# Masks of the first scores as two constant operand rows and triangles of 64; first loads dealt anew; new orders

## The chip, the cores and the metric

The kernel runs on one core of a Trainium2 chip. The metric is the device time of one execution in microseconds (us), the median of three runs. The engines are TensorE (PE, matrix products), VectorE (DVE), ScalarE (ACT), GpSimd (POOL) and SyncE (SP), which here only issues transfers.

## The reference

Four residual steps on x of 4 batches x 256 tokens x 128 features:

```python
x = x + tanh(g_xattn[0]) * xattn0(layernorm(x), ctx, ctx, ...)   # 16 heads of 8, masked
x = x + tanh(g_ffn[0])   * ffn0(layernorm(x), ...)               # top-1 of 6 low-rank token factors
x = x + tanh(g_xattn[1]) * xattn1(layernorm(x), ctx, ...)        # 8 heads of 64
x = x + tanh(g_ffn[1])   * ffn1(layernorm(x), ...)               # top-2 of 8 experts, then a layer norm
```

The change touches the mask of the first attention. A token sees only tokens before it, and token 0 sees itself:

```python
scores = jnp.einsum('bihd,bjhd->bhij', qh, kh) * scale
keep = (j < i) | (i == 0) & (j == 0)
scores = jnp.where(keep, scores, jnp.float32(-jnp.inf))
probs = jax.nn.softmax(scores, axis=-1)
```

## The kernel before

Each engine runs a list written out by hand: `PE_ORDER`, `ACT_ORDER`, `DVE_ORDER`, `POOL_ORDER` and `SP_ORDER`. An entry such as `S:6` names a function and its arguments. An engine takes its list strictly in order and waits on semaphores where data or a buffer is missing.

PSUM has three pairs of banks that are used in turn by the entries in `PAIRED` (projections `pk`, keys and values `kv`, scores `S`, transposed scores `T` and others), so an entry waits until the entry three places before it in that ring has been read. One bank (`misc`) serves transposes and small products, one the attention outputs.

The first attention works like this. `xT:0:b` transposes the normalised x of batch b, `pk:b` projects the context to keys and values, `pq:b` the queries. Queries and keys are split in three bf16 parts each (`hi`, `sres`, `mid`, `lo`), so that a float32 product becomes one bf16 product over six planes of 8 features, 48 rows (`KR`). The parts go through a scratch tensor in memory: `so:b:part` on SP writes them (two transfers for each part), `si:b` waits for all of them and reads them back as one head per block of columns, eight heads on rows 0 to 47 and eight on rows 64 to 111.

Scores are computed twice. First `S:n`, 24 groups, six for each batch (`UNITS`): rows are queries, and VectorE (`mx:n`) takes the negated row maxima out of them. For this pass TensorE first writes the mask into the diagonal block of each bank, as an identity times a mask tile (line 1092), and adds the score products on top (line 1097). Groups with it=1 hold the queries 128 to 255 (two heads of 256 columns in a bank, two masks of 256 columns), groups with it=0 the queries 0 to 127 (four heads of 128 columns, two masks of 512 columns). `mparts:b` splits the maxima in two bf16 parts, `mT:b` transposes them, `MTc:b` copies them, and two transfers (`shift:b` on SP, one on ACT) put them in as two more operand rows, 48 and 49; the keys have rows of ones there. Then `T:n:i` (lines 1112 and 1116) computes the transposed scores with the maxima subtracted, ScalarE exponentiates (`e0`), GpSimd zeroes the masked triangle (`mask:n`), and `AV:n` multiplies with the values.

`hT`, `oT` and `wo0` carry the heads to the output projection, `awo0` adds to x. The first feed-forward runs over `gate`, `yk`, `ym` (mask times factors), `lg` (logits), `pte`, `U` and `val`; the second attention over `q`, `sc`, `tp` and `av1`, with keys and values from the context by `kv:b:0` and `kv:b:1`; the experts are `hid` and `eo`.

SP loads x, the context and weights at the start, ACT the constants and the small tables of the first feed-forward (`COL`, `BTG`, `WTD`, `AA`, `BW`).

Of the kernel before, what the change touches and what calls it, by code (L numbers as in the profile page):

```python
# [34 lines left out]
KS = KR + 2  # L35
# [9 lines left out]
C_ID, C_MASK, C_W6 = 0, 128, 384  # L45
NCONST = 390
# [10 lines left out]
xT:0:0 pk:0 pq:0 xT:0:1 pk:1 pq:1 tok:0 kv:0:0 xT:0:2 kv:0:1 pk:2 pq:2 xT:0:3 pk:3 pq:3 kv:1:0 kv:1:1 S:0 S:1  # L57
S:2 S:3 S:4 S:5 kv:2:0 S:6 S:7 mT:0 S:8 S:9 kv:2:1 S:10 T:0:0 S:11 T:0:1 T:1:0 T:1:1 S:12 mT:1 AV:0 T:2:0 T:2:1
S:13 AV:1 S:14 T:3:0 T:3:1 hT:0 AV:2 S:15 T:4:0 S:16 AV:3 T:4:1 S:17 T:5:0 hT:1 T:5:1 T:6:0 S:18 S:19 mT:2 AV:4
T:6:1 S:20 oT:0 T:7:0 S:21 wo0:0 T:7:1 AV:5 T:8:0 S:22 T:8:1 AV:6 T:9:0 hT:2 T:9:1 S:23 xT:1:0 AV:7 gate:0  # L60
T:10:0 T:10:1 AV:8 T:11:0 hT:3 yk:0 mT:3 AV:9 tok:1 oT:1 lg:0 T:11:1 wo0:1 kv:3:0 hT:4 pte:0 T:12:0 AV:10 xT:1:1
# [62 lines left out]
def build_program(nc, x, ctxT, w0, wo0, btg, aa, wtd, vecs, cols, w1, wo1, wr, bias, w12, consts,  # L124
# [6 lines left out]
    with ctx:  # L131
# [20 lines left out]
        MSKB = sb("MSKB", [P, 2, P], bf16)  # L152
# [21 lines left out]
        ONE = sb("ONE", [2, S], bf16)  # L174
# [100 lines left out]
        d_one, s_one = map(sem, ("d_one", "s_one"))  # L275
# [48 lines left out]
        def _(sp):  # L324
# [80 lines left out]
        def _(pool):  # L405
# [4 lines left out]
            g_.memset(ONE[:, :], 1.0).then_inc(s_one, 1)  # L410
# [82 lines left out]
        def _(act):  # L493
# [86 lines left out]
            def maxima_rows(b):  # L580
# [385 lines left out]
        def _(pe):  # L966
# [113 lines left out]
            def scores0(n):  # L1080
# [20 lines left out]
            def scores0T(n, i):  # L1101
# [299 lines left out]
```

## Time and profile before

| | |
|---|---|
| median of the runs | 204.18 us (203.66 to 204.18) |
| the profiled execution, its own time | 204.24 us |
| its span, first to last instruction | 202.2 us |
| busy: PE, DVE, ACT, POOL | 181.8, 142.5, 122.7, 105.4 us |
| chain that ended last, by engine | PE 60%, DVE 19%, DMA 5%, ACT 4% |

The profile is one execution. Busy is the time in which an engine had an instruction running; matmuls are pipelined, so a busy TensorE is not one at its peak. In the views a row gives the start in us from the span's beginning, the busy time, engine, line of the kernel, operation, the tile written and read with shapes, the number of instructions, and in brackets how long the engine had been idle before, and what released it.

### The profile page before, as it was taken

The page shows a single profiled execution, that of the slowest core. Times are in us where ns is not written, and L with a number is a line of the kernel's source. Part 1 is how long each engine was busy: PE and PEld are TensorE (multiplying, and loading weights), DVE is VectorE, ACT ScalarE, POOL GpSimd, SP SyncE. Part 2 cuts the span into 40 slices and gives each one's busy share as a digit, 9 for nine tenths or more (in the row PEclk, how much of TensorE's full clock was granted, in tenths as well). Part 3 has the DMA queues.
Part 4 walks back from the last instruction along what each step waited for, and adds up shares of the span by engine and source line. Part 5 has one row for each costly group of instructions (what it writes and reads, how often), then busy time and mean ns, then how long its engine had stood idle before and what let it go on. Part 6 is the DMA issues. An engine that isn't in the chain of part 4 may idle for free.

```text
span 202.2 us, 4352 instructions
## 1 busy us (share of the span) xinstructions
PE 181.8 (90%) x1516; PEld 128.4 (64%) x1516; DVE 142.5 (70%) x361; ACT 122.7 (61%) x313; POOL 105.4 (52%) x153
## 2 busy tenths in 40 slices
PE   0799789799999999999898999999999899999990
PEld 0588244254456857465675877667867679998980
DVE  1684499877996465678878585795798755857744
ACT  0665402777687795676795568788776737255250
POOL 7420000275457446594555938896695955095302
PEclk9999999999999999999999999999999999999999
DMA  5968994854000000000000000000006107347101
GB/s 97 342 188 228 284 206 104 243 132 63 8 5 0 3 3 0 0 3 0 3 0 3 0 3 0 0 3 0 0 2 181 58 3 233 110 130 200 60 26 52
DMA packets 14744, 15.04 MB, mean 74 GB/s; under 512 B 1695, under 2 KB 12164, under 8 KB 14724
## 3 DMA queue, kind: packets, MB, share of 16 engines
q1 hardware_dynamic: 13676, 14.28, 26.4%
q10 hardware_dynamic: 1048, 0.50, 1.1%
q8 instruction: 12, 0.20, 0.4%
q14 instruction: 8, 0.07, 0.1%
HBM read 10.98 MB, written 3.67 MB: 72 GB/s over the span
## 4 chain that ended last, share of the span: by engine, by line
PE 60%; DVE 19%; DMA 5%; ACT 4%; SPq 3%; POOL 3%; issue 3%; POOLq 0%; DVEq 0%; ACTq 0%
PE PS L1319 7%; PE PS L1329 7%; DVE MX L754 6%; PE PS L1135 6%; PE PS L1258 6%; PE PS L1287 5%; PE PS L1271 4%; DMA POOLED<-qk_scr 3%; ACT POOLED L650 3%; PE PS L1092 3%; PE PS L1299 3%; DVE XH L722 3%; DVE NM L857 2%; SPq L352 2%; DMA W<-in_w 2%
## 5 line engine op out<-in xcount | busy, mean ns | idle before, releaser
L458 POOL TENSOR_TENSOR POOLED<-POOLED,RC 128x512 f32<-128x512 f32 x32 | 32.8, 1047 | 13.9 <-DVE RC L866 13.9
L650 ACT ACTIVATE POOLED<-PS,NM 128x256 f32<-128x256 f32 x64 | 29.4, 480 | 7.0 <-DVE NM L857 5.1
L754 DVE TENSOR_REDUCE MX<-PS 128x4 f32<-128x1024 f32 (+1 forms) x24 | 28.5, 1221 | 6.8 <-PE PS L1097 6.6
L447 POOL TENSOR_SCALAR_AFFINE_SELECT PT<-PT 128x512 f32<-128x512 f32 x16 | 10.2, 638 | 41.0 <-ACT PT L570 41.0
L570 ACT ACTIVATE PT<-PS 128x768 f32<-128x768 f32 x32 | 24.8, 809 | 4.8 <-PE PS L1116 4.7
L857 DVE TENSOR_REDUCE NM<-PS 128x4 f32<-128x1024 f32 x16 | 19.4, 1218 | 3.5 <-PE PS L1258 3.2
L722 DVE TENSOR_SCALAR XH<-X,MV,RS 128x128 f32<-128x128 f32 x32 | 15.8, 536 | 4.8 <-POOL RS L416 4.8
L681 ACT ACTIVATE POOLED<-PS,BI 128x256 f32<-128x256 f32 x32 | 12.6, 475 | 10.7 <-PE PS L1319 8.7
L1258 PE MATMUL PS<-KT,VA 64*128 64x256 f32 x128 | 17.9, 400 | 0.1
L415 POOL TENSOR_SCALAR VE<-MV 128x2 f32<-128x2 f32 x20 | 5.3, 267 | 24.2 <-DVE MV L707 12.9
L1271 PE MATMUL PS<-CST,POOLED 128*128 128x128 f32 x128 | 17.1, 276 | 0.1
L1287 PE MATMUL PS<-POOLED,V 128*64 128x256 f32 x128 | 16.6, 389 | 0.0
L1271 PEld LDWEIGHTS PS<-CST,POOLED 128*128 128x128 f32 x128 | 14.1, 141 | 3.2 <-issue 2.3
L1329 PEld LDWEIGHTS PS<-POOLED 128*128 128x128 f32 x128 | 14.8, 192 | 1.4 <-issue 1.1
L1329 PE MATMUL PS<-POOLED 128*128 128x128 f32 x128 | 15.6, 278 | 0.2
L416 POOL TENSOR_TENSOR RS<-VE,HALF 128x2 f32<-128x2 f32 x20 | 14.6, 731 | 1.7
L1319 PE MATMUL PS<-XT,POOLED 128*128 128x256 f32 x64 | 14.9, 382 | 0.0
L1135 PE MATMUL PS<-PT,VA 128*32 128x256 f32 (+1 forms) x256 | 13.8, 331 | 0.0
L1033 PE MATMUL PS<-CST,XH 128*128 128x128 f32 x32 | 7.0, 303 | 7.6 <-DVE XH L722 6.7
L650 ACT ACTIVATION_READ_ACCUMULATOR POOLED<-PS,NM 128x1 f32 x64 | 13.6, 212 | 0.0
L1258 PEld LDWEIGHTS PS<-KT,VA 64*128 64x128 f32 x128 | 11.2, 186 | 3.5 <-issue 1.9
L1092 PE MATMUL PS<-MSKB,IDB 128*128 128x256 bf16 (+1 forms) x48 | 11.1, 312 | 2.3 <-DMA POOLED<-qk_scr 1.2
(146 smaller groups left out, 383.1 us busy)
## 6 DMA issues: line engine op xcount, KB each, us to landing
POOLED<-in_w SPq DMA_DIRECT2D x8, 512.0 KB, 4.0
POOLED<-qk_scr SPq DMA_DIRECT2D x8, 384.0 KB, 6.0
qk_scr<-POOLED SPq DMA_DIRECT2D x8, 192.0 KB, 2.4
qk_scr<-POOLED SPq DMA_DIRECT2D x8, 128.0 KB, 2.2
W<-in_w SPq DMA_DIRECT2D x3, 256.0 KB, 5.8
BI<-in_bias SPq DMA_DIRECT2D x8, 66.0 KB, 3.7
qk_scr<-POOLED SPq DMA_DIRECT2D x8, 64.0 KB, 2.6
out_x<-X SPq DMA_DIRECT2D x4, 128.0 KB, 1.8
```

Of the source, the lines that this page charges most:

```text
L458: g_.tensor_tensor(pr, pr, RC1[:, n % 2, 2 * h:2 * h + 2].unsqueeze(2).to_broadcast([P, 2, S]), ALU.mult).then_inc(s_p1p, 1)
L570: a.activation(PT0[:, n % 3, i:4:2, :], pair("T", n, i).rearrange("p (r n) -> p r n", r=2)[:, :, 0:384], ACT.Exp, scale=D0 ** -0.5).then_i ...
L650: last = a.activation(PR[n % 3][:, h, it, :], pair("sc", n)[:, h * 512 + it * S:h * 512 + (it + 1) * S], ACT.Exp, bias=NM1[:, n % 2, 2 * h ...
L722: last = v.tensor_scalar(XH[:, t, :], X[:, t, :], MV[:, t, 0:1], RS[:, t:t + 1], ALU.subtract, ALU.mult)
L754: v.tensor_reduce(MX0[:, b, it, :, hw * k:hw * (k + 1)], pair("S", n).rearrange("p (r h j) -> p r h j", r=2, h=hw), AXX, ALU.max, negate=T ...
L857: v.tensor_reduce(NM1[:, k, :], pair("sc", n).rearrange("p (c j) -> p c j", j=S), AXX, ALU.max, negate=True).then_inc(s_nm1, 1)
L1135: last = mm(banks(6)[rows, half + jt * P:half + S], VA[:, 2 * b + jt, 4 * hg + g, :], src, start=(jt == 0), stop=(jt == 1), skip_group_che ...
L1258: last = mm(bank[:, h * 512 + it * S:h * 512 + (it + 1) * S], QT1[rows, b % 2, c, it * P:(it + 1) * P], KT1[rows, c, b * S:(b + 1) * S], s ...
L1271: last = nc.tensor.transpose(bank[:, at:at + P], PR[n % 3][:, h, it, jt * P:(jt + 1) * P], ident)
L1287: last = mm(banks(6)[rows, (n % 2) * S:(n % 2 + 1) * S], V1[:, 2 * b + jt, (2 * c + h) * D1:(2 * c + h + 1) * D1], PT1[n % 3][:, h, jt, :] ...
L1319: last = mm(bank[:, f * S:(f + 1) * S], W12[m][:, f * P:(f + 1) * P], XT[:, b * S:(b + 1) * S], start=True, stop=True)
L1329: last = mm(bank[:, 512 * t:512 * t + P], HT[:, m % 2, f, t * P:(t + 1) * P], W12[m][:, F + f * P:F + (f + 1) * P], start=(f == 0), stop=( ...
```

## The change

Five things are done.

1. The mask of the first scores is no longer a full 128 x 128 block on the diagonal. Only the two triangles of 64 on the diagonal are added by products with an identity (64 rows each, the two banks of a pair taking rows 0 to 63 and 64 to 127; `SHIFTED` is the identity with its halves swapped). The 64 x 64 square above the diagonal between them is masked by two further operand rows of the scores: on the query side ones in a quarter of the tokens, on the key side -1e30 in the next quarter. The score products so have 50 rows (`KM`) in place of 48, the transposed ones 52 (`KS`) in place of 50. The maxima move to rows 50 and 51.
2. These rows and the rows of ones come from a new tensor in memory, `rows`, by four transfers (`constant_rows`); before, two transfers took the ones from a tile that GpSimd had set.
3. ACT starts with two loads in place of eight. The mask constants go to SP (`cm`), the tables of the first feed-forward to SP after the output weights (`te`). W0 goes ahead of the context, x:1 behind the first of the key and value weights, W1:0 and the last context ahead of the first scratch read.
4. The orders of all five engines are new.
5. The ODT copy of batch 0 waits for `COL` itself, since `COL` is now loaded late.

```diff
+KM = KR + 2
+KS = KM + 2
+HP = P // 2
...
+            def constant_rows():
+                for side, n in ((1, 4), (0, 2)):
+                    for r in range(2):
+                        sp.dma_start(BIGF[64 * r + KR:64 * r + KR + n, 4096 * side:4096 * (side + 1)].rearrange(
+                            "p (b n) -> p b n", b=B),
+                            rows[side, 0:n].unsqueeze(1).to_broadcast([n, B, H0 * S // 4])).then_inc(d_one, 16)
...
+                a.activation(SHIFTED[:, 0:HP], ident[:, HP:P], ACT.Copy)
+                a.activation(SHIFTED[:, HP:P], ident[:, 0:HP], ACT.Copy)
...
-                for r in range(2):
-                    diag = bank[:, r, :].rearrange("p (h j) -> p h j", h=hw)[:, :, w - P:w]
-                    mm(diag, IDB[:, :], MSKB[:, it:it + 1, :].to_broadcast([P, hw, P]),
-                       start=True, stop=False, skip_group_check=True)
+                for half in range(2):
+                    for r in range(2):
+                        rows = slice(HP * r, HP * (r + 1))
+                        part = bank[:, r, :].rearrange("p (h j) -> p h j", h=hw)[:, :, w - P + HP * half:w - HP + HP * half]
+                        which = MSKB[rows, max(it, half):max(it, half) + 1, :].to_broadcast([HP, hw, HP])
+                        mm(part, (IDB, SHIFTED)[(half + r) % 2][rows, :], which, start=(half == 0), stop=False,
+                           skip_group_check=True)
                 for g in range(hw):
                     for r in range(2):
-                        rows = slice(64 * r, 64 * r + KR)
+                        rows = slice(64 * r, 64 * r + KM)
...
+    for k in range(2):
+        half[0, k] = np.where(quarter == 2 * k, one, 0)
+        half[1, k] = np.where(quarter == 2 * k + 1, low, 0)
...
-x:0 x:1 c:0 w0 x:2 c:1 w1:1 w1:2 c:2 so:0:0 so:0:1 so:0:2 so:1:0 so:1:1 so:1:2 si:0 so:2:0 so:2:1 so:2:2 si:1
+x:0 w0 c:0 cm w1:1 x:1 w1:2 x:2 one c:1 so:0:0 so:0:1 so:0:2 w1:0 c:2 si:0 so:1:0 so:1:1 so:1:2 so:2:0 so:2:1
```

Three places of the lists, as the built programs have them. First SP from its start to the first scratch read, before and then after. `qk_scr` is the scratch tensor, `CT` the context, a `W` of 384 columns W0 and one of 512 a part of W1.

```order
L330 DMA X<-in_x 128x2x128 x2
L333 DMA CT<-in_ctxT 128x256
L336 DMA W<-in_w 128x384
L330 DMA X<-in_x 128x4x128
L333 DMA CT<-in_ctxT 128x256
L339 DMA W<-in_w 128x512 x2
L333 DMA CT<-in_ctxT 128x512
L352 DMA qk_scr<-POOLED 128x3x256 x2
L352 DMA qk_scr<-POOLED 128x2x256 x2
L352 DMA qk_scr<-POOLED 128x256 x2
...
L361 DMA POOLED<-qk_scr 48x2x2048 x2
```

```order
L347 DMA POOLED<-in_rows 4x4x1024 x2
L347 DMA POOLED<-in_rows 2x4x1024 x2
L335 DMA CT<-in_ctxT 128x256
L366 DMA qk_scr<-POOLED 128x3x256 x2
L366 DMA qk_scr<-POOLED 128x2x256 x2
L366 DMA qk_scr<-POOLED 128x256 x2
L341 DMA W<-in_w 128x512
L335 DMA CT<-in_ctxT 128x512
L375 DMA POOLED<-qk_scr 48x2x2048 x2
```

Before, the writes of batches 0 and 1, twelve transfers, stand ahead of the first read; after, six writes and two loads.

Second, TensorE from the third transpose up to the first two score groups, before and after. L1033 becomes L1043 (transpose), L1042, L1044 and L1051 become L1052, L1054 and L1061 (pk and pq), L1072 and L1077 become L1082 and L1087 (keys, values), L1092 and L1097 become L1107 and L1112 (masks, scores).

```order
L1033 MATMUL PS<-CST,XH 128x128 x2
L1042 MATMUL PS<-CT,W 128x256
L1044 MATMUL PS<-W,CT 128x128 x2
L1051 MATMUL PS<-XT,W 128x256
L1072 MATMUL PS<-CT,W 128x256 x4
L1077 MATMUL PS<-W,CT 128x512 x2
L1092 MATMUL PS<-MSKB,IDB 128x2x128 x2
L1097 MATMUL PS<-POOLED 128x256 x4
```

```order
L1043 MATMUL PS<-CST,XH 128x128 x2
L1052 MATMUL PS<-CT,W 128x256
L1054 MATMUL PS<-W,CT 128x128 x2
L1061 MATMUL PS<-XT,W 128x256
L1082 MATMUL PS<-CT,W 128x256 x4
L1087 MATMUL PS<-W,CT 128x512 x2
L1107 MATMUL PS<-MSKB,IDB 128x2x64
L1107 MATMUL PS<-MSKB,SHIFTED 128x2x64 x2
L1107 MATMUL PS<-MSKB,IDB 128x2x64
L1112 MATMUL PS<-POOLED 128x256 x4
```

Before, these are batch 3's transpose and projection and batch 1's keys and values; after, batch 2's transpose and projection and batch 2's keys and values. A mask of two products with 256 columns is now four with 128.

Third, VectorE behind the first six maxima, before and after. L754 becomes L764 (maximum), L763 and L764 become L773 and L774 (`mparts`); L746, L751 and L756 are `sres`, `mid` and `lo` of batch 3, which before stood ahead of the first maximum.

```order
L754 TENSOR_REDUCE MX<-PS 128x2x4
L763 CAST MP<-MX 128x4x8
L764 TENSOR_TENSOR MP<-MX,MP 128x4x8
L754 TENSOR_REDUCE MX<-PS 128x2x2 x2
L754 TENSOR_REDUCE MX<-PS 128x2x4
L754 TENSOR_REDUCE MX<-PS 128x2x2 x2
```

```order
L764 TENSOR_REDUCE MX<-PS 128x2x4
L746 TENSOR_TENSOR PT<-PS,POOLED 128x512
L773 CAST MP<-MX 128x4x8
L774 TENSOR_TENSOR MP<-MX,MP 128x4x8
L751 CAST POOLED<-PT 128x2x256
L764 TENSOR_REDUCE MX<-PS 128x2x2 x2
L764 TENSOR_REDUCE MX<-PS 128x2x4
L764 TENSOR_REDUCE MX<-PS 128x2x2 x2
L756 TENSOR_TENSOR POOLED<-PT,POOLED 128x2x256
```

The split of batch 3 now stands among the maxima.

## Rows read from the trace of the kernel before

**Rows 1.** The page, parts 1 and 2: busy, and TensorE's granted clock.

```profile
PE 181.8 (90%) x1516; PEld 128.4 (64%) x1516; DVE 142.5 (70%) x361; ACT 122.7 (61%) x313; POOL 105.4 (52%) x153
...
PEclk9999999999999999999999999999999999999999
```

**Rows 2.** The chain that ended last: start us, us, what.

```profile
17.28 6.06 DMA POOLED<-qk_scr
...
24.33 6.89 DVE MX L754 x6
```

**Rows 3.** Windows: length, busy PE, PEld, DVE, ACT, POOL, clock, DMA share, GB/s.

```profile
24.33:66.48 42.15, 39.15 (x474) 19.80 (x472) 36.03 (x54) 24.51 (x36) 17.13 (x30) 1.00 0.43 99
66.48:162.00 95.52, 90.96 (x737) 65.51 (x733) 70.16 (x176) 69.95 (x215) 65.36 (x84) 1.00 0.05 14
```

**Rows 4.** Waits: engine, line, released by: us in total, times, longest.

```profile
DVE MX L754 <- PE PS L1097: 6.6, 10, 2.7
```

**Rows 5.** Timeline of PE up to the first scores.

```profile
8.78 1.06 PE L1051 MATMUL PS<-XT,W 128*128 128x256 f32 x2
...
12.09 1.92 PE L1072 MATMUL PS<-CT,W 128*128 128x256 f32 x8
13.85 0.38 PE L1033 MATMUL PS<-CST,XH 128*128 128x128 f32 x2
14.06 1.88 PE L1077 MATMUL PS<-W,CT 128*128 128x512 f32 x4
15.78 0.59 PE L1042 MATMUL PS<-CT,W 128*128 128x256 f32 x2
...
16.66 0.60 PE L1051 MATMUL PS<-XT,W 128*128 128x256 f32 x2
17.09 0.38 PE L1033 MATMUL PS<-CST,XH 128*128 128x128 f32 x2
...
23.58 0.38 PE L1092 MATMUL PS<-MSKB,IDB 128*128 128x256 bf16 x2 [1.22 <-DMA POOLED<-qk_scr]
```

**Rows 6.** Timeline of SP around the first scratch read.

```profile
10.50 6.24 SPq L352 DMA_DIRECT2D qk_scr<-POOLED  x12
16.79 0.92 SPq L361 DMA_DIRECT2D POOLED<-qk_scr  x2
```

**Rows 7.** DMA issues: number, KB each, median us from issue to landing.

```profile
qk_scr<-POOLED SPq DMA_DIRECT2D x8, 192.0 KB, 2.4
...
CT<-in_ctxT SPq DMA_DIRECT2D x1, 256.0 KB, 6.1
```

**Rows 8.** Timeline, ACT's first work.

```profile
4.59 1.28 ACT L514 ACT_TABLE_LOAD   x1 [4.59 <-issue]
```

**Rows 9.** Timeline of PE later in the scores, and behind them.

```profile
57.54 0.39 PE L1092 MATMUL PS<-MSKB,IDB 128*128 128x256 bf16 x2
57.86 0.39 PE L1097 MATMUL PS<-POOLED 48*128 48x256 bf16 x4
...
60.27 0.60 PE L1092 MATMUL PS<-MSKB,IDB 128*128 128x512 bf16 x2
60.81 0.40 PE L1097 MATMUL PS<-POOLED 48*128 48x128 bf16 x8
61.14 0.44 PE L1033 MATMUL PS<-CST,XH 128*128 128x128 f32 x2
...
67.04 0.59 PE L1206 MATMUL PS<-AA,YM 96*128 96x100 f32 x4
...
72.50 0.27 PE L1112 MATMUL PS<-POOLED 50*128 50x256 bf16 x2
...
72.67 0.27 PE L1112 MATMUL PS<-POOLED 50*128 50x256 bf16 x2
```

**Rows 10.** Groups by line, DVE, 10 to 24 us: busy, mean ns | idle before.

```profile
L736 DVE TENSOR_TENSOR PT<-PS,POOLED 128x512 f32<-128x512 f32 x4 | 2.8, 688 | 3.5 <-ACT POOLED L529 3.5
L741 DVE CAST POOLED<-PT 128x512 bf16<-128x512 f32 x4 | 1.7, 427 | 0.1
```

More of the change, by code:

```diff
@@ L56 @@
 PE_ORDER = table("""
[L57 to L61, printed above, removed]
@@ new lines @@
+T:6:0 S:18 mT:2 S:19 T:6:1 AV:5 T:7:0 S:20 S:21 xT:1:0 T:7:1 AV:6 T:8:0 gate:0 T:8:1 T:9:0 S:22 AV:7 hT:2 yk:0
+T:9:1 tok:0 hT:3 lg:0 S:23 T:10:0 oT:1 tok:1 wo0:1 pte:0 T:10:1 U:0 mT:3 val:0 T:11:0 xT:1:1 AV:8 gate:1 T:11:1
+AV:9 T:12:0 T:12:1 yk:1 hT:4 AV:10 AV:11 T:13:0 T:13:1 lg:1 xT:2:0 q:0 hT:5 pte:1 T:14:0 oT:2 U:1 T:14:1 sc:0
+val:1 wo0:2 sc:1 AV:12 T:15:0 sc:2 AV:13 xT:1:2 T:15:1 gate:2 AV:14 tp:0 sc:3 yk:2 xT:2:1 AV:15 hT:6 q:1 lg:2
+tp:1 sc:4 hT:7 tp:2 sc:5 oT:3 av1:0 wo0:3 pte:2 tp:3 av1:1 U:2 sc:6 xT:1:3 val:2 gate:3 av1:2 tp:4 yk:3 av1:3
@@ L82 @@
+log0:3 e1:8 ot:2 pta:7 e1:9 e1:10 pta:8 xTc:2:3 ot:3 e1:11 pta:9 qc:3 pta:10 e1:12 ot:4 e1:13 pta:11 xTc:3:1
+e1:14 pta:12 ot:5 e1:15 gelu:0 pta:13 pta:14 ot:6 xTc:3:2 pta:15 ot:7 gelu:1 xTc:3:3 gelu:2 gelu:3 gelu:4 gelu:5
+gelu:6 gelu:7
 """)
 DVE_ORDER = table("""
-st:0:0 ln:0:0 st:0:1 ln:0:1 st:0:2 st:0:3 sres:0 mid:0 lo:0 ln:0:2 sres:1 mid:1 lo:1 ln:0:3 sres:2 mid:2 lo:2
-sres:3 mid:3 lo:3 mx:0 mx:1 mx:2 mx:3 mx:4 mx:5 mparts:0 mx:6 mx:7 mx:8 mx:9 mx:10 mx:11 mparts:1 mx:12 mx:13
-mx:14 hn:0 mx:15 mx:16 mx:17 mparts:2 hn:1 mx:18 mx:19 mx:20 mx:21 awo0:0 mx:22 ln:1:0 hn:2 mx:23 gat:0 mparts:3
@@ L93 @@
-ptd:14 ptd:15 ridx:1 rl:2 awo1:3 base:0 rwk:1 ridx:2 ln:3:3 fin:0 fin:1 rl:3 base:1 ridx:3 fin:2 out:0 rwk:2
-fin:3 base:2 fin:4 rwk:3 fin:5 out:1 base:3 fin:6 out:2 fin:7 out:3
+st:0:0 ln:0:0 st:0:1 sres:0 mid:0 lo:0 ln:0:1 st:0:2 st:0:3 ln:0:2 sres:1 mid:1 ln:0:3 lo:1 sres:2 mid:2 lo:2
+mx:0 mx:1 mx:2 mx:3 mx:4 mx:5 sres:3 mparts:0 mid:3 mx:6 mx:7 mx:8 mx:9 mx:10 lo:3 mx:11 mparts:1 mx:12 mx:13
+mx:14 hn:0 mx:15 mx:16 hn:1 mx:17 mparts:2 awo0:0 mx:18 mx:19 ln:1:0 mx:20 mx:21 gat:0 mx:22 hn:2 ym:0 hn:3
@@ new lines @@
+smx:0 mx:23 nrm:0 awo0:1 mparts:3 um:0 ln:1:1 gat:1 add0:0 hn:4 ym:1 ln:2:0 smx:1 nrm:1 hn:5 um:1 nm:0 awo0:2
+nm:1 rc:0 ln:1:2 nm:2 add0:1 gat:2 rc:1 ln:2:1 nm:3 ptd:0 ym:2 hn:6 rc:2 smx:2 ptd:1 rc:3 nm:4 hn:7 nrm:2 nm:5
+ptd:2 awo0:3 ptd:3 ln:1:3 rc:4 um:2 nm:6 gat:3 rc:5 ptd:4 rc:6 ym:3 add0:2 smx:3 nm:7 nrm:3 ln:2:2 awo1:0 ptd:5
+rc:7 um:3 ln:3:0 ptd:6 nm:8 ptd:7 nm:9 rc:8 add0:3 nm:10 rc:9 ln:2:3 rl:0 ptd:8 nm:11 rc:10 ridx:0 rc:11 ptd:9
+awo1:1 nm:12 ptd:10 nm:13 rc:12 ptd:11 ln:3:1 nm:14 rc:13 ptd:12 rl:1 rwk:0 nm:15 ptd:13 rc:14 ridx:1 rc:15
@@ L95 @@
+awo1:2 ptd:14 ln:3:2 ptd:15 rwk:1 base:0 rl:2 base:1 ridx:2 awo1:3 fin:0 ln:3:3 fin:1 rl:3 ridx:3 out:0 rwk:2
+base:2 fin:2 fin:3 fin:4 fin:5 rwk:3 out:1 base:3 out:2 fin:6 fin:7 out:3
 """)
 POOL_ORDER = table("""
-vaset rstd:0:0 rstd:0:1 rstd:0:2 rstd:0:3 mask:0 mask:1 vecp mask:2 mask:3 bias:0:0 mask:4 mask:5 mask:6
-rstd:1:0 mask:7 bias:0:1 mask:8 mask:9 mask:10 mask:11 rstd:1:1 mask:12 bias:0:2 mask:13 pexp:0 ws:0 rstd:1:2
-rstd:2:0 pexp:1 bias:0:3 ws:1 mask:14 mask:15 rstd:2:1 norm:0 norm:1 rstd:1:3 norm:2 norm:3 norm:4 pexp:2
@@ L104 @@
+mask:14 pexp:1 rstd:1:2 ws:1 bias:0:3 norm:0 rstd:2:1 mask:15 norm:1 norm:2 norm:3 rstd:1:3 norm:4 pexp:2 ws:2
+norm:5 rstd:2:2 bias:1:0 norm:6 norm:7 rstd:3:0 pexp:3 ws:3 norm:8 rstd:2:3 norm:9 r1b:0 norm:10 bias:1:1
+norm:11 rstd:3:1 r1c:0 norm:12 bias:1:2 norm:13 r1b:1 norm:14 norm:15 rstd:3:2 r1c:1 r1b:2 bias:2:0 bias:1:3
+rstd:3:3 r1c:2 r1b:3 bias:2:1 rstd:4:0 bias:2:2 rstd:4:1 r1c:3 rstd:4:2 bias:2:3 rstd:4:3
 """)
 SP_ORDER = table("""
-x:0 x:1 c:0 w0 x:2 c:1 w1:1 w1:2 c:2 so:0:0 so:0:1 so:0:2 so:1:0 so:1:1 so:1:2 si:0 so:2:0 so:2:1 so:2:2 si:1
@@ L108 @@
-wo:0 one si:2 shift:0 so:3:0 so:3:1 vec so:3:2 wo:1 w1:0 shift:1 si:3 shift:2 shift:3 w12:0 w12:1 w12:2 w12:3
-outd:0 outd:1 outd:2 outd:3
+x:0 w0 c:0 cm w1:1 x:1 w1:2 x:2 one c:1 so:0:0 so:0:1 so:0:2 w1:0 c:2 si:0 so:1:0 so:1:1 so:1:2 so:2:0 so:2:1
+si:1 so:2:2 vec so:3:0 shift:0 si:2 so:3:1 wo:0 so:3:2 shift:1 si:3 wo:1 te shift:2 shift:3 w12:0 w12:1 w12:2
+w12:3 outd:0 outd:1 outd:2 outd:3
 """)
@@ L1354 @@
     c[:, C_ID:C_ID + P] = np.eye(P, dtype=fp)
-    row, col = np.mgrid[0:P, 0:P]
+    row, col = np.mgrid[0:P, 0:HP]
+    row = row % HP
     for it in range(2):
         keep = (col < row) | ((row == 0) & (col == 0) & (it == 0))
-        c[:, C_MASK + it * P:C_MASK + (it + 1) * P] = np.where(keep, fp(0), fp(-BIG))
+        c[:, C_MASK + it * HP:C_MASK + (it + 1) * HP] = np.where(keep, fp(0), fp(-BIG))
     c[:, C_W6:C_W6 + 6] = np.arange(NX, 0, -1, dtype=fp)
+    one, low = (int(np.array(v, fp).view(np.uint32)) >> 16 for v in (1.0, -BIG))
+    quarter = np.arange(S) // HP
+    half = np.full((2, 4, H0 // 2, S), one, np.uint16)
+    for k in range(2):
+        half[0, k] = np.where(quarter == 2 * k, one, 0)
+        half[1, k] = np.where(quarter == 2 * k + 1, low, 0)
+    rows = half.reshape(2, 4, H0 * S // 2).view(fp)
     aa = np.zeros((NL, NL + NER + 2), fp)
@@ L1388 @@
         "consts": c,
+        "rows": rows,
     }
```

90 lines of the change are left out of this document (39 added, 51 removed).

## The prediction

> **What bounds the kernel now.** I read the page first: TensorE is busy for 181.8 of 202.2 us, at a granted clock of full speed in every slice [rows 1]. A share over the whole span says little here, so the next view is the chain that ended last. It starts with loads and the split, waits 6.06 us for the first scratch read, and then runs through six row maxima of VectorE in a row, 6.89 us [rows 2]. The reader is to see there that TensorE does not set the pace once the scores begin. The third view is the table of windows: from the first maximum (24.33) to the mask times factors of the first feed-forward batch (66.48), VectorE is busy 36.03 of 42.15 us and TensorE 39.15 [rows 3]. Almost all of VectorE's idle time there is a maximum that waits for its scores: 6.6 us over the kernel, of which the longest wait, 2.7, lies ahead of the first one [rows 4]. So this stage is a braid of two nearly full engines, each of which waits for the other. Later, up to 162 us, TensorE is the fuller one: 90.96 of 95.52 us [rows 3].
>
> **Change 1, work moved ahead of the scores.** Before, TensorE ends kv:1:1 about 22.4 and waits 1.22 us for scratch [rows 5]. Now kv:2:0 and kv:2:1 also stand ahead of S:0, while xT:0:3, pk:3 and pq:3 go behind it. I read costs start to start [rows 5]: transpose 0.21 (13.85 to 14.06), pk 0.88 (15.78 to 16.66), pq 0.43 (16.66 to 17.09), keys 1.75 (12.09 to 13.85), values 1.72 (14.06 to 15.78). The first pq took 1.06 us busy against 0.60 for the same two instructions at 16.66, with the granted clock at full speed in both; up to about 11 us everything ran at half rate, and I price that as it is.
> W0 now leaves SP second, one issue slot (0.5 us) earlier, so xT, pk:0 and pq:0 run back to back from 6.18 and end at 9.78 instead of 9.86. Behind it stand kv:0:0 (1.75, and 0.55 more for the slow 1.1 us), kv:0:1 1.72, xT:0:1 0.21, kv:1:0 1.75, pk:1 and pq:1 1.31, kv:1:1 1.72, xT:0:2 0.21, pk:2 and pq:2 1.31, kv:2:0 1.75, kv:2:1 1.87 (its busy time, as nothing follows that overlaps): 14.2 us, so S:0 starts at 24.0 against 23.58. This start is 0.4 late but has 3.6 us more work behind it. The scratch read hides under it: the SP queue held twelve split writes of 0.52 us each ahead of it (6.24 us from 10.50, read issued at 16.79) and now holds six, two loads of 0.46 each, as the two reads took, and the landing of the last split write. Six issues end about 13.7, plus 2.4 to land is 16.1; with 6.55 from issue to landing (16.79 to 23.34, the end of the wait on the chain) it is there at 22.7 [rows 2, 6, 7]. Were that cover gone, each late microsecond would move S:0.
> The constant rows (four small loads) and c:1 are issued by 8 us; TensorE wants c:1 at 13.8, and the 256 KB load of that kind took 6.1 us [rows 7], so they cost nothing. c:2 leaves at about 14.6, lands about 20.7 by that row, and pk:2 wants it at 19.1 in my walk: up to 1.6 us could show, bounded from below by nothing, since that landing was measured with all weights in flight. I take 0 and keep 1.6 for the range. ACT loses six issues ahead of its first table load, which starts at 4.59 [rows 8]. What it frees is the copy of xT ahead of pq:0, and pq:0 stands behind pk:0 on TensorE anyway, so I price it at 0.
>
> **Change 2, the masks.** A score group of the second token tile costs 0.32 us of mask (57.54 to 57.86) and 0.32 of scores; one of the first tile 0.54 (60.27 to 60.81) and 0.33 [rows 9]. The masks are two 128-row products of 256 or 512 columns that run one after the other. The scores are four of 256 columns on rows 0 to 47 and 64 to 111, and take 0.32 us, in which one after the other would not fit, 1024 columns being 0.43 us at 2.4 GHz, the level of the granted clock: the halves run side by side. The new masks are four 64-row products of 128 or 256 columns, of the form of the scores, so I price them by the scores: half of 0.21, 0.11, and half of 0.42, 0.21. Besides, a T pair (384 columns) that follows another T costs 0.17 (72.50 to 72.67), which is its columns at full rate, while scores behind a 128-row mask take 0.32 for 0.21 us of columns [rows 9]: 0.11 us goes at each change between the two kinds. With mask and scores of one kind, one such step per group falls away. By the same clock 512 columns are 0.21 us. So a group goes from 0.64 to 0.43 and from 0.87 to 0.54: 16 times 0.21 and 8 times 0.33 is 6.0 us of TensorE.
> The Trainium skill (TensorEngine Tiling, Key Properties) says that a change of the tiling mode drains TensorE, while different tiles may load and multiply in parallel; the trace agrees with both, as 0.11 us a change. Without that rule's step saved, the sum by halved columns alone would be about 3.4 us in place of 6.0. The bound on the other side, four products one behind the other with a load of 0.05 each, is 0.63 us per mask of the first tile and 0.42 of the second, a loss of 2.3 us.
>
> **Where this lands.** TensorE is not the one to ask. From S:0 to lg:0 it took 43.5 us (23.58 to 67.04) less 3.0 idle [rows 3, 5, 9] = 40.5. Now: less kv:2 (3.6), less the masks (5.8 of 6.0), plus batch 3's projection (1.5), plus kv:3, which came after lg:0 and now stands among the scores (3.5), less what now comes after lg:0 (S:23 0.54, three T 0.6, AV:8 and AV:9 1.6, mT:3, tok:1 and oT:1 1.0, together 3.7): 32.5, to 56.5. VectorE: 36.03 busy [rows 3], less the last maximum, one mparts and one hn (1.22, 0.38, 0.54), plus sres:3, mid:3, lo:3, now behind the maxima (0.69, 0.43, and 0.69 like the first [rows 10]): 35.7. The first maximum starts one group (0.43) and 0.1 after S:0, at 24.53, so VectorE cannot pass that point before 60.2. Two waits are built in: S:6 stands behind mT:0, which waits for mparts:0 (0.5 us), and the mask copy before ym:0 (0.5 us before). That is 61.2. Before, VectorE idled 6.1 us in this stretch; I leave a fourth of it, 1 us more than the walk has, so lg:0 at 62.2 against 67.04: 4.8 us, with as much TensorE work behind it within 0.2 (3.5 in, 3.7 out). The rest, 135 us, I leave as it is: it runs on the same instructions, and only 4.6 us of its TensorE time up to 162 is idle. Span 197.4, and the 2.04 us around it (204.24 less 202.2) make 199.4; the runs' median of 204.18 is the same thing within 0.1.
>
> **Rivals.** (a) The rest shrinks too. Attention 2's first score now stands ahead of AV:12, where it stood behind AV:13, so its softmax starts with more slack. Half of the 4.6 us idle goes: 197.1. For it: VectorE has that slack to give. Against: nothing of before's trace shows that those waits come from a late start.
> (b) The masks do not run side by side: 2.3 us lost instead of 6.0 won puts TensorE at 64.7, behind VectorE; with its own waits 65, so 2.0 us gain: 202.2. Against: the score rows.
> (c) Slower: scratch reads with too little lead. si:2 now stands behind shift:0 and si:3 behind shift:1 on SP. mT:0 comes at 32.6, shift:0 at 33.3, si:2 at 34.0, landed 40.5; S:12 is wanted at about 41.0. mT:1 at 42, si:3 43.4, landed 50.0; S:18 wanted at 51. Slack is 0.5 and 1.0, and what exceeds it is paid in full by VectorE. At 10 us of landing for each, 3.45 more than measured, 2.95 and 2.45 go: 204.8. It decides once the two are together 4.8 us late; c:2's 1.6 helps it.
> (d) No change: lg:0 comes early, and FFN batches 1 to 3, later now in TensorE's list against attention 2, give it back: 204.
>
> **The numbers.** Forecast 0.5, for itself 198.4 to 200.8; (a) 0.18; (b) 0.14; (c) 0.11; (d) 0.07. What a measurement can tell from no change is 0.3%, 0.6 us. Faster 0.82, same 0.07, slower 0.11. The range leaves out (c), (d) and the far side of (a): 196.3 to 203.0.
>
> **What would show it.** S:0 at 24.0 with no wait for scratch; a group's masks 0.11 and 0.21 us, and no gap between mask and scores; VectorE nearly gapless from 24.5; lg:0 near 62; kv:3 among S:5 to S:8. Wrong would be: the first maximum after 26, VectorE waiting for scores at S:12 or S:18 with a scratch read as releaser, or a second half longer than 135 us from lg:0.

## The result, and the profile after

The changed kernel takes 209.38 us (median of 4 runs, 208.12 to 210.06) against 204.18 us (203.66 to 204.26). The ratio is 1.024, 95% interval 1.020 to 1.027: slower, where 199.4 us was forecast. The profiled execution took 210.06 us with a span of 208.0 us. Medians of later comparisons each have the kernel before beside them; it stayed at 204.27 to 204.35 us. A ratio leaves disturbed executions out and a median does not, which is why the two differ for e11, where four of six are left out.

The page of after, busy time and the 40 slices:

```profile
PE 181.6 (87%) x1564; PEld 131.8 (63%) x1564; DVE 145.6 (70%) x361; ACT 122.0 (59%) x315; POOL 103.8 (50%) x152
...
PEclk9999999759959999999999999999999999999998
```

TensorE's busy time is 181.6 us, against 181.8 in [rows 1]: the 6 us of mask columns that were taken out are not missing from it. The row of the clock says why: instructions that run at half rate take longer. The granted clock, at full speed in every slice of [rows 1], has two dips. Timeline of PE of after at the first scores and at the first masks of the second tile:

```profile
23.95 0.23 PE L1107 MATMUL PS<-MSKB,IDB 64*128 64x128 bf16 x1
...
24.07 0.38 PE L1112 MATMUL PS<-POOLED 50*128 50x256 bf16 x4
24.30 0.22 PE L1107 MATMUL PS<-MSKB,IDB 64*128 64x128 bf16 x1
...
35.33 0.28 PE L1107 MATMUL PS<-MSKB,IDB 64*128 64x256 bf16 x1
...
35.56 0.39 PE L1112 MATMUL PS<-POOLED 50*128 50x128 bf16 x8
```

The start of the scores and the cost of a mask are as forecast: S:0 at 23.95, and a group from 23.95 to 24.30, 0.35 us, of which the mask is 0.12 and the scores 0.23, for 0.32 each [rows 9]. The larger mask takes 0.23 (35.33 to 35.56), where it took 0.54 before [rows 9]. The trouble comes later. Windows of PE of after: length, busy, granted clock, DMA share, GB/s:

```profile
36.00:39.00 3.00, 2.03 (x32) 1.00 1.03 217
39.00:40.00 1.00, 0.46 (x4) 0.57 0.95 109
40.00:45.00 5.00, 3.83 (x48) 0.50 0.31 85
...
55.00:57.00 2.00, 0.00 (x0) 0.80 0.23 59
57.00:63.00 6.00, 5.62 (x54) 0.50 0.00 0
63.00:64.00 1.00, 1.00 (x30) 0.98 0.06 16
```

From about 39.1 to 46.0 and from about 56.2 to 63.1 the granted clock is 0.50, its lower level of 1.2 GHz (the row of 39.00 to 40.00 is a mean over the fall at 39.1, the row of 55.00 to 57.00 one over the fall at 56.2). Each time TensorE had been idle for part of the time just before. Two new waits stand there. First, timeline of VectorE and then of ScalarE:

```profile
39.40 0.91 DVE L756 TENSOR_TENSOR POOLED<-PT,POOLED 128x512 bf16<-128x512 f32 x1
...
42.28 1.23 DVE L764 TENSOR_REDUCE MX<-PS 128x8 f32<-128x1024 f32 x1 [1.97 <-PE PS L1112]
```

```profile
40.34 3.07 ACT L578 ACTIVATE PT<-PS 128x768 f32<-128x768 f32 x4 [1.87 <-DVE POOLED L756]
```

`e0:1:0` on ScalarE waits 1.87 us for `lo:3` (line 756), which the new VectorE list puts behind mx:6 to mx:10. The exponentials wait because, at that entry, the code asks for all four low parts (the remainders that the low parts are made from lie in the buffer `PT0` that the exponentials fill). TensorE, whose bank ScalarE holds, cannot make S:11, and VectorE then waits 1.97 us for it. Timeline of TensorE there:

```profile
39.54 0.40 PE L1125 MATMUL PS<-POOLED 52*128 52x256 bf16 x2 [0.63 <-DVE MX L764]
...
41.20 0.39 PE L1107 MATMUL PS<-MSKB,IDB 64*128 64x256 bf16 x1 [1.17 <-ACT PT L578]
```

The clock falls at 39.1, in the gap of 0.63 us that a maximum ends. The 1.17 us that ScalarE costs TensorE come after it, so that wait did not start the first stretch at half rate. Second, the chain that ended last (start us, us, what), SP's queue up to the column table:

```profile
46.82 0.40 SPq L375
...
47.97 0.43 SPq L385
...
48.92 7.81 DMA COL<-in_cols
...
56.81 0.48 ACT ODT L603
57.29 0.09 issue
57.38 1.19 PE PS L1187 x4
```

The waits, us in total, times, longest:

```profile
DVE MX L764 <- PE PS L1112: 5.9, 6, 2.0
DVE X L791 <- PE PS L1187: 3.9, 1, 3.9
PE PS L1187 <- ACT ODT L603: 3.9, 1, 3.9
ACT ODT L603 <- DMA COL<-in_cols: 3.7, 1, 3.7
```

The tables of the first feed-forward and of the output bias left the start of ACT for a late place in SP's list, behind shift:1, si:3 and wo:1. `COL` is issued at 48.92 and lands 7.81 us later, `oTc:0` wants it 3.7 us before that, and TensorE stands still at wo0:0 for 3.9 us. lg:0 comes at 71.23 against 67.04 [rows 9]. From there to the end of the span it is 136.8 us, against 135.2 before.

### The profile page after: what moved, and what is told of

Same layout as the page of the kernel before. It is cut to its first block, busy times and chain, and to the rows that moved or that the text cites. A ratio compares the mean times of both kernels' runs of the same rounds, so it can differ in the third digit from the quotient of the medians.

```text
span 208.0 us, 4451 instructions
## 1 busy us (share of the span) xinstructions
PE 181.6 (87%) x1564; PEld 131.8 (63%) x1564; DVE 145.6 (70%) x361; ACT 122.0 (59%) x315; POOL 103.8 (50%) x152
## 4 chain that ended last, share of the span: by engine, by line
PE 59%; DVE 22%; POOL 6%; DMA 5%; issue 3%; ACT 2%; SPq 1%; POOLq 0%; DVEq 0%; ACTq 0%
PE PS L1284 6%; PE PS L1342 5%; PE PS L1332 5%; DVE XH L732 5%; DVE MX L764 5%; PE PS L1300 5%; PE PS L1271 4%; DMA COL<-in_cols 4%; PE PS L1257 4%; PE PS L1148 3%; PE PS L1087 3%; PE PS L1082 3%; PE PS L1312 3%; POOL RS L429 2%; PE PS L1043 2%
## 5 line engine op out<-in xcount | busy, mean ns | idle before, releaser
L764 DVE TENSOR_REDUCE MX<-PS 128x4 f32<-128x1024 f32 (+1 forms) x24 | 28.3, 1219 | 6.3 <-PE PS L1112 6.1
L578 ACT ACTIVATE PT<-PS 128x768 f32<-128x768 f32 x32 | 25.4, 810 | 10.0 <-PE PS L1129 6.8
L732 DVE TENSOR_SCALAR XH<-X,MV,RS 128x128 f32<-128x128 f32 x32 | 16.7, 565 | 8.0 <-POOL RS L429 8.0
L1148 PE MATMUL PS<-PT,VA 128*32 128x256 f32 (+1 forms) x256 | 14.9, 361 | 0.1
L1043 PE MATMUL PS<-CST,XH 128*128 128x128 f32 x32 | 6.8, 296 | 9.2 <-DVE XH L732 8.4
L517 ACT ACTIVATE XT<-PS 128x256 f32<-128x256 f32 x16 | 6.1, 384 | 14.6 <-PE PS L1043 14.5
```

The lines of the kernel that those rows point to most:

```text
L578: a.activation(PT0[:, n % 3, i:4:2, :], pair("T", n, i).rearrange("p (r n) -> p r n", r=2)[:, :, 0:384], ACT.Exp, scale=D0 ** -0.5).then_i ...
L732: last = v.tensor_scalar(XH[:, t, :], X[:, t, :], MV[:, t, 0:1], RS[:, t:t + 1], ALU.subtract, ALU.mult)
L764: v.tensor_reduce(MX0[:, b, it, :, hw * k:hw * (k + 1)], pair("S", n).rearrange("p (r h j) -> p r h j", r=2, h=hw), AXX, ALU.max, negate=T ...
L1148: last = mm(banks(6)[rows, half + jt * P:half + S], VA[:, 2 * b + jt, 4 * hg + g, :], src, start=(jt == 0), stop=(jt == 1), skip_group_che ...
```

## The experiments

**e1: the tables early.** In SP's list the entry `te` goes from behind wo:1 to behind c:1.

```diff
-one c:1 so:0:0 ... wo:1 te shift:2
+one c:1 te so:0:0 ... wo:1 shift:2
```

> Changed kernel with one edit: the five small tables (te: COL, BTG, WTD, AA, BW) are issued on SP behind c:1, ahead of the first split write, where SP is free from 6.75 to 9.99 us. Theory 1 (late COL): the copy oTc:0 no longer waits 3.7 us for COL, the second stretch at half clock (56 to 63 us) does not come, and the time falls by 3.7 us plus 1 to 3 us of TensorE work at half rate: 203.5 to 205. Rival (another wait takes its place): VectorE's maxima or the scratch reads set the pace there anyway, the time falls by under 2 us, to 207.5 or more. The first stretch at half clock (39.6 to 46) should stay by both.

Measured 205.05 us, ratio 1.0035 (1.0002 to 1.0069). lg:0 comes at 65.8, 136.8 us before the end. Windows of all engines (busy of PE, PEld, DVE, ACT, POOL, then the clock):

```profile
42.00:46.00 4.00, 3.92 (x54) 2.06 (x52) 2.80 (x4) 2.63 (x5) 2.44 (x4) 0.58 0.07 17
56.00:63.00 7.00, 6.58 (x112) 3.73 (x112) 6.47 (x13) 5.82 (x10) 4.04 (x8) 1.00 0.02 6
```

The wait and the half-rate stretch behind it are gone, the first stretch stays, shorter and later (about 42.6 to 46.0): 4.3 us hang on the place of five small transfers.

**e8: the wait kept, its clock mended.** The kernel after with 64 products of 128 columns ahead of wo0:0, which are overwritten later.

```diff
+                if b == 0:
+                    for _ in range(64):
+                        mm(banks(6)[:, 0:P], IDB[:, :], IDB[:, :], start=True, stop=True)
                 take_misc("wo0", b)
```

> The changed kernel as it is, with 64 products of 128x128 by 128 columns (about 3.5 us, results overwritten) ahead of wo0:0, that is in the wait for the late column table. Parts the wait from the clock behind it. Theory (the 3.7 us wait and then some 6 us at half clock both count): the wait stays at 3 us or more, the half-rate stretch of 56 to 63 us goes, lg:0 comes 1.5 to 3 us earlier than 71.24 and the time is 206 to 208 us. Rival (the wait alone counts; the half-rate stretch lies beside VectorE's work): 209 to 210 us with lg:0 at 71.

Measured 207.27 us, ratio 1.0145 (1.0112 to 1.0178), lg:0 at 69.0. Timeline and windows of PE:

```profile
53.27 3.75 PE L1184 MATMUL PS<-IDB 128*128 128x128 bf16 x64
57.30 0.68 PE L1190 MATMUL PS<-WO,ODT 128*128 128x128 f32 x4 [0.28 <-ACT ODT L603]
```

```profile
57.00:63.00 6.00, 5.30 (x89) 1.00 0.03 7
```

ScalarE still waits 3.8 us for `COL`, yet the four products of wo0:0 take 0.68 us where they took 1.19, and the time falls by 2.1 us. Of the 4.3 us of e1, about half was the wait (2.2) and half the clock that it left behind (2.1).

**e2 and e3: the low part early, alone and with the tables.**

```diff
-mid:3 mx:6 mx:7 mx:8 mx:9 mx:10 lo:3 mx:11
+mid:3 lo:3 mx:6 mx:7 mx:8 mx:9 mx:10 mx:11
```

> Changed kernel with one edit: lo:3 stands right behind mid:3 on VectorE, ahead of mx:6, and no longer behind mx:10. Theory 2 (e0:1:0 waits for lo:3): ScalarE's wait of 1.9 us for the low part at 38.5 to 40.3 goes, S:11 comes 2 us earlier, the first stretch at half clock (39.6 to 46 us) goes too, and everything behind moves up 2 to 4 us, the issue of COL with it: 205.5 to 207.5. Rival (the clock falls because TensorE has little to do between maxima anyway): the wait goes, the clock still falls, gain under 1.5 us: 208 or more.

> Changed kernel with both edits, tables early and lo:3 early. Theory 1 and 2 together: both waits and both stretches at half clock go; lg:0 at 62 to 64 us instead of 71.2, time 199.5 to 202.5, below the kernel before. Rival (the rest of the new orders is worse than the old ones, masks aside): 203.5 or more.

e2 measured 206.75 us, ratio 1.0113 (1.0077 to 1.015): 2.6 us less than after, as expected. In its profiled execution, at 204.91 us the fastest of ten, the clock is full from 24 to 54 us, and falls only behind the wait for `COL`. e3 measured 203.73 us, ratio 0.9951 (0.9916 to 0.9986), barely faster than before, outside my range for it and inside the rival's. Its ten runs spread with the granted clock: 202.6 and 202.81 us at 0.999 and 0.996, 204.69 to 205.08 at 0.977 to 0.983. In the profiled one (203.0 us of span, S:0 at 24.9, lg:0 at 66.3) no wait for the tables or the low part is left, and the clock still falls, twice (at 29.1 and 42.7). Windows of PE of e3:

```profile
24.00:35.00 11.00, 9.52 (x79) 0.84 1.02 239
35.00:46.00 11.00, 9.35 (x118) 0.85 0.68 140
```

**e4 and e5: the masks alone.** e4 has the five lists and ACT's loads of before and only the new mask (with its rows loaded ahead of the first split write). e5 issues each of its mask products twice.

```diff
-                        mm(part, ..., which, start=(half == 0), stop=False, ...)
+                        for _ in range(2):
+                            mm(part, ..., which, start=(half == 0), stop=False, ...)
```

> The new masks alone: all five orders and the loads on ACT as before, except that the constant rows are loaded ahead of the first split write. Theory (the score stage is bound by VectorE and TensorE in turn): a score group costs 0.35 to 0.54 us instead of 0.64 and 0.87, TensorE's work falls by about 6 us, and the time by 1.5 to 3.5, to 200.7 to 202.7. Rival a (TensorE is what binds from 41 us on): the whole 4 to 5 us show, 199.5. Rival b (less TensorE work between maxima lets the clock fall): a stretch at half clock appears and the time is 204 or more.

> The kernel of e4 (new masks, old orders), with each of the four mask products of a score group issued twice, so that TensorE streams about as long per group as with the full masks; the mask value is then -2e30 in one half, which changes no result. Theory (the granted clock falls because TensorE has too little to do between two maxima): the clock stays at 0.99 or above in 24 to 46 us, where e4 had 0.963 over the run, and the time is 203.5 to 205.0 us, not above e4's 205.58 although TensorE has some 5 us more work. Rival (TensorE's work in this stage simply counts, the clock falls for another reason): 206 to 209 us, clock still below 0.98.

e4 measured 205.58 us, ratio 1.0038 (1.0011 to 1.0066), at clocks of 0.963 to 0.982 in all ten runs; e5 203.79, ratio 0.9968 (0.9948 to 0.9988), at 0.984 to 0.998. Windows of PE, e4 and then e5:

```profile
24.00:34.00 10.00, 9.17 (x78) 0.53 0.89 190
34.00:41.00 7.00, 5.44 (x64) 0.94 0.55 123
41.00:46.00 5.00, 4.21 (x62) 0.66 0.58 163
```

```profile
24.00:34.00 10.00, 8.96 (x134) 0.83 1.01 213
34.00:41.00 7.00, 5.20 (x74) 1.00 0.59 154
41.00:46.00 5.00, 4.45 (x87) 1.00 0.73 192
```

Smaller masks in the old orders make the kernel slower, as rival (b) of e4 said, and more TensorE work makes it faster again, by 1.8 us between two comparisons. The two kernels differ in nothing but that work, and what it changed for the better is the clock. What starts e4's first stretch has another source. In both kernels TensorE waits 2.0 us ahead of S:0, before 1.22 [rows 5]; in e5 the clock fell after it too, but was back in 3.4 us instead of 10. The expectation of 0.99 or above from 24 to 46 us was therefore too high: the rows of e5 give 0.92. That e5 beats the kernel before by 0.5 us I did not trace.

**e6, e7 and e9: more TensorE work in the new orders.** e6 is e3 with all mask products twice; e9 only in groups 0 to 11; e7 is e3 with the full masks of before.

```diff
-                        for _ in range(2):
+                        for _ in range(2 if n < 12 else 1):
```

> The kernel of e3 (new masks and orders, tables and last low part early), with the mask products issued twice. Clock theory: the half-rate stretches between 29 and 47 us go, the mean clock is 0.99 or more in all runs, and the time is 202.0 to 203.3 us, at or below e3's 203.73. Rival: the clock is not set by this work, and 24 groups with 0.2 us more each cost 1 to 4 us: 204.7 to 208 us.

> The mask of before (full 128 rows and columns, ones rows written from SBUF) in the new orders, with the tables and the last low part early as in e3: the orders alone. Theory 1 (the small masks are worth next to nothing here, because VectorE's maxima bound the stage and the clock falls when TensorE idles): within 0.5% of e3, 202.8 to 204.7 us, at a clock of 0.99 or more. Rival (the small masks carry the gain and the new orders need them): 205.5 to 208 us.

> The kernel of e3 with the mask products issued twice in the first twelve score groups only (those up to 47 us, where TensorE waits for the maxima); the last twelve, where TensorE has no idle time to speak of, have the small masks once. Clock theory: the clock stays at 0.99 or more and the later groups keep their 0.2 us each: 201.8 to 203.4 us, at least 1 us below e6's 204.80 and not above e3's 203.73. Rival (doubling costs what it adds wherever it stands, or the clock is only moved to another stretch): 204 to 205.5 us.

Measured: e6 204.80 us (ratio 1.002, 0.9986 to 1.0054), e7 206.63 (1.0115, 1.0075 to 1.0154), e9 203.64 (0.9955, 0.9922 to 0.9989). On e7 my theory was wrong and the rival right: with the same orders and early entries, the full masks cost 2.9 us more than the small ones (e3). So the small masks are worth something in these orders even with the clock's share taken off: from S:0 to lg:0 the profiled e7 takes 43.95 us and e9 40.2, both at a full clock. The new orders with the old masks lose 2.3 us. e6 lies in the rival's range, and five of its twelve executions had a clock below 0.99, where none was expected. In e6 and e9 the profiled clock is full through the scores, but their medians are no better than e3's: e9's gain over e6 is there (1.2 us, at least 1 was expected), a gain over e3 is not, and 203.64 lies 0.2 above the range that the clock theory gave. So in the new orders no median shows a gain from a fuller clock. The profiled e9, 202.7 us with its surroundings, shows what is left when neither waits nor clock disturb. Windows of PE up to lg:0 and from there:

```profile
24.00:63.80 39.80, 35.11 (x526) 1.00 0.56 122
63.80:200.70 136.90, 125.68 (x1017) 0.99 0.14 40
```

And the same of e3:

```profile
24.00:66.20 42.20, 37.55 (x485) 0.92 0.60 126
66.20:203.00 136.80, 125.52 (x1017) 1.00 0.14 40
```

lg:0 comes 2.4 us earlier in e9. Only half of that is the clock's to explain: S:0 is already at 24.93 in this execution of e3 and at 23.68 in e9, since the keys and values of batch 0 took 1.0 us longer and the load of c:1 was waited for 0.3 us longer. From S:0 to lg:0 it is 41.3 us at 0.92 against 40.2 at full clock, although e9's first twelve groups carry extra products. The rest is the same length. Why other executions of e9 took up to 205.72 us, at a clock of 0.987, stays open: only one of them was profiled.

**e10: the old orders, masks twice in twelve groups.** The same line in the kernel of e4.

> The same with the old orders: the kernel of e4 with the mask products twice in the first twelve score groups only. Clock theory: as e5 or better by the 12 later groups at 0.2 us each where TensorE is the bound: 202.0 to 203.6 us, clock 0.985 or more. Rival (the half-rate stretch of 41 to 46 us comes back because groups after the twelfth are small again): 204.5 to 205.6 us with a clock of 0.96 to 0.975.

Measured 204.09 us, ratio 0.9972 (0.9944 to 1.0), clocks 0.977 to 0.999, between the two expectations. Windows of PE:

```profile
24.00:35.00 11.00, 9.98 (x143) 0.84 0.78 176
35.00:46.00 11.00, 9.11 (x126) 0.84 0.67 187
```

The second stretch at half rate came back in part; in e5, with all masks doubled, the clock is full from 35 to 46. That it is a matter of which groups are small is not shown: the clock fell at 41.2, and of the groups ahead of that only S:12 (40.0) is small in e10 and not in e5, some 0.1 us of work. One execution of each was profiled, and e10's clocks range from 0.977 to 0.999.

**e11 and e12: new front, old rest.** e11 is e3 up to S:22 and behind it the order of before on all four engines; e12 doubles the masks of its first twelve groups.

```diff
 S:20 S:21 xT:1:0 T:7:1 AV:6 T:8:0 gate:0 T:8:1 T:9:0 S:22
-AV:7 hT:2 yk:0 T:9:1 tok:0 hT:3 lg:0 S:23 T:10:0 oT:1 ...
+tok:0 hT:2 T:9:1 S:23 AV:7 T:10:0 T:10:1 AV:8 T:11:0 hT:3 yk:0 ...
```

> The kernel of e3 up to S:22 on TensorE (e0:9:0 on ScalarE, mx:22 on VectorE, mask:9 on GpSimd), all that comes behind in the order of the kernel before. Theory (the new orders idle TensorE 1.5 us more behind lg:0, 136.8 us from lg:0 to the end against 135.2, and this belongs to the order of the second half alone): lg:0 at 66 to 67 us, 135.0 to 135.6 us from there to the end, median 201.8 to 203.0 us. Rival (the second half takes longer because the front hands it over in another state, kv:3 done and the transposed products behind): no gain, 203.4 to 205 us.

> The kernel of e11 with the mask products issued twice in the first twelve score groups: both remedies together. If both theories hold, 200.5 to 202.3 us at a clock of 0.99 or more, the fastest of all; if only the one on the clock, 202.5 to 203.5; if only the one on the orders, as e11 within 0.3%.

Neither theory's numbers: 209.34 us (1.0108, 1.0032 to 1.0183; its six executions spread from 205.6 us at a clock of 0.99 to 212.28 at 0.95) and 210.04 (1.0268, 1.0227 to 1.031). Timeline of PE of e12 at the seam, and its windows:

```profile
80.34 0.71 PE L1188 MATMUL PS<-WO,ODT 128*128 128x128 f32 x4
83.24 0.40 PE L1229 MATMUL PS<-CST,TE 128*100 128x128 f32 x2 [2.18 <-DVE TE L844]
```

```profile
78.00:84.00 6.00, 3.82 (x39) 1.00 0.01 3
84.00:94.00 10.00, 9.82 (x47) 0.51 0.00 0
```

The cut made a new wait of 2.18 us at pte:1, and ten microseconds at half clock followed, with TensorE 98% busy all through. The part from lg:0 on is 138.7 us (68.75 to 207.5); e11 has the same wait, 2.2 us, and the same half-rate stretch. So the question whether the longer second half belongs to its order alone was not answered; what the pair shows is a third wait with the same train behind it, in another stage.

## Why the prediction was wrong

**The start of the scores: right, and in part by luck.** S:0 at 23.95 for 24.0, without a wait for scratch. But kv:0:0 ran longer than priced (3.03 us on the chain for 2.30), and it began 0.45 us earlier on the chain (9.33 for 9.78); the two errors nearly cancel. c:1, priced at nothing, was not waited for in this execution; in the profiled ones of e3, e8, e9, e11 and e12 it was, for 0.3 to 1.1 us.

**The masks: right, a little better than priced.** 0.35 us for a group of the second tile (0.43 was forecast) and 0.23 us for the larger mask (0.21). The mask is as priced, 0.12 for 0.11; the scores behind it went from 0.32 to 0.23 us too, which the walk had left at 0.32. "The halves run side by side" holds, and rival (b) falls with it. (Its load of 0.05 us a product stands in no row; the weight loads of the masks before took 0.10 us each, beside other products.) What the masks are worth in the new orders is e7 less e3, 2.9 us, where 5.8 us of TensorE work were taken out in the walk.

**"TensorE is not the one to ask": one step that failed.** The walk took VectorE's busy time, added known waits and 1 us, and left TensorE's speed at what the trace of before had. But making TensorE lighter in a stage where it waits for another engine can make its clock fall. In the old orders this is shown: e4 is 0.4% slower than the kernel before, e5, with more work, 0.3% faster. In the new orders the profiled executions point the same way (0.92 from 24 us to lg:0 in e3, 1.00 in e6, e7 and e9), and the medians do not show it. The profile before had numbers to be asked about, 39.15 of 42.15 us [rows 3] and a clock that never fell [rows 1]: the change takes away some of the work beside which the clock was full. The Trainium skill (TensorE: Matmul & The Clock Gate, A second HAM failure mode: psum-queue depth-cycling) says that short idle times between groups of products can make the clock go back and forth. It does so here in e3 (0.84 and 0.85 in the two stretches of 11 us) and e4 (0.53, 0.94, 0.66); e9, with extra products at 1.00, agrees with it from the other side. I had no rival for it.

**ACT's freed issues, "I price it at 0": the step that failed by most, with the low part two waits never priced.** The prediction counts ACT's six freed issues as 0 and does not ask where they went. SP's list puts them behind si:3 and wo:1; by its own rows, an entry there leaves SP after 43.4 and takes some 6 us to land, against an `oTc:0` whose place the list also shows. That is worth 4.3 us (e1), 2.2 of it the wait and 2.1 the clock behind it (e8). The `lo:3` behind five maxima was in the sum as 0.69 us of VectorE's work, not as a thing that e0:1:0 waits for: 2.6 us (e2), 1.3 us once the tables are early (e3 against e1). These two waits are 5.7 of the 10.0 us between forecast and measurement (e3 against after), and they turn a kernel that is 0.5 us faster than before into a slower one.

**Rival (c): not what happened.** The slower case was rightly looked for on SP, but at the scratch reads. si:2 left at 34.5 and no maximum or score showed a wait for a scratch read; the 0.11 for slower was too little for a list of new orders in which only some of the entries had been walked.

**The walk to lg:0 and the rest.** At full clock and without the two waits lg:0 is at 63.85 (e9, with half of the masks doubled; e6 with all of them 64.9), 62.2 was forecast. VectorE was busy 35.4 us (35.7 forecast) and idle 3.9 us where I had allowed 2. The trace before was read too kindly there: of the 6.1 us that VectorE idled from 24.33 on, not almost all but 3.9 (6.6 less the 2.7 ahead of the first maximum, [rows 4]) were maxima waiting for scores. "The rest, 135 us, I leave as it is" was wrong by 1.6 us: 136.6 to 136.9 in every kernel with the new orders (after, e1, e2, e3, e6, e7, e8, e9), 135.0 to 135.2 in every one with the old (before, e4, e5, e10), with TensorE's busy time equal within 0.5 us. The new second half has more idle time, and why stays open; rival (a) had it shrink. The sum in order: 199.4 forecast, 1.6 for lg:0 and 1.7 for the rest give 202.7, the profiled e9; 1.0 more gives e3's median, 203.73, and is what is left for the clock in the scores and for executions that start late (the profiled e3, 205.1, has 2.3 more, of which 1.25 is its late S:0). Then 1.3 us for the low part (e1, 205.05) and 4.3 us for the tables make after.

## What to carry to other kernels

In a stage where TensorE and another engine wait for each other in turn, price a cut of TensorE's work together with its clock: look whether the granted clock is full, and how near to full TensorE is beside it, before counting the columns as won. A wait on TensorE can be paid twice, once itself and once in the half rate behind it: here one of 3.9 us cost 4.3 us of the kernel's time, about half of it by the clock (e1, e8). When a change deals transfers anew, follow each one of them from its new place to its first reader, the small ones too, for here five small tables cost 4.3 us in a kernel that, with both waits mended, is 0.5 us faster than before.

## What was not expected of the hardware

The clock stays at its lower level while TensorE is nearly full: 98% busy for 10 us at 0.51 (e12), 9.17 of 10 us at 0.53 (e4). So a high busy share beside a low clock is a slow engine and no sign of a full one. Sixty-four small products, 3.75 us whose results nobody reads, made the kernel 2.1 us faster (e8). A table of 1 KB, `COL`, took 7.81 us from issue to landing behind a scratch read and two weight loads, and 7.2 to 8.3 us when it was issued early on SP (e1, e3, e9), where it had taken 4.4 on ACT before; a small transfer is not a quick one. The clock can fall at a smaller idle time than one it withstands elsewhere: in the kernel before it stays full through a gap of 0.91 us at 97 us, in the changed one it falls in a gap of 0.63 us at 39.1. And the clock is not all: e6 took 203.95 us in one execution and 205.62 in another, both at a clock of 1.0. What parts them was not found.
